# Placing VectorE's small steps by weight in a hand-planned two-layer transformer kernel

## The chip, the cores and the metric

One core of a Trainium2 chip. The metric is the device time in microseconds of one execution; the kernel before took 1615.34 us (median of three runs).

## The reference, cut to what matters

Input x is (4, 1024, 128) float32. There are two layers; each adds an attention branch and a feed-forward branch to x, and both branches read the same layer norm. Layer 0: rotary attention (16 heads of 8), and a mixture of 8 experts with the top 2 per token. Layer 1: causal attention without rotation, and a feed-forward whose inputs and weights are rounded blockwise (blocks of 16) to the FP4 grid.

```python
xn = _layernorm(x, axis=-1)
x = x + _L0_attn_ref(xn, ...) + _L0_ffn_ref(xn, ...)   # softmax(QK^T/sqrt(8))V Wo; top-2 of 8 experts, 128->512->128
xn = _layernorm(x, axis=-1)
x = x + _L1_attn_ref(xn, ...) + _L1_ffn_ref(xn, ...)   # causal; fp4(silu(fp4(xn) Wg) * (fp4(xn) Wu)) Wd
```

## The kernel before, in words

The work is cut into eight **phases** (layer, batch): (0,0) (0,1) (1,0) (0,2) (1,1) (0,3) (1,2) (1,3), numbered 0 to 7. A phase's attention is a row of **steps** (head group g of four heads, half qh of the queries, key tile kt of 128): 64 in a layer-0 phase, 48 in a causal one. Beside the steps run **quads**, 12 slots ahead of them and so often already of the next phase: they compute the same scores the other way round, only to find each query's maximum.

A class `Plan` (lines 42 to 325) writes the whole program out by hand before anything is emitted, as a list of **slots**. One slot holds at most one step, one quad, the product with V of the step before ("pv"), and lists of extra pieces. Every engine walks through the same slots in order:

- TensorE: two heads of the step's scores and of the quad's, the eight matmuls of pv into the bank pO, the other two heads, then the extra pieces ("xs"). All results but pO's go into a ring of seven PSUM banks; TensorE waits until the bank it wants has been emptied. All matmuls are emitted by the helpers on lines 521 (matmul) and 524 (transpose).
- ScalarE: exp of the four score tiles (L833), and its share of the xs copies.
- VectorE: two maxima (L1180 in full, L1184 with the causal mask), the small steps of positions 0 and 1, two maxima, at the end of a head group the combination of the maxima (L1416 to L1419), the small steps of position 2, its share of the xs evictions, the small steps of position 3.
- GpSimd: in order, rstd (L731), sum, rem and lo of the split of Q and K into three bf16 parts (L738, L742, L746), eight rounding operations of the FP4 step at two a slot (L790 to L810), scatter and gather of the expert rows (L763, L779).
- SyncE: all other DMAs, in slot order, each with its waits.

**Extra pieces (xs)**, by who evicts them. ScalarE: xT (transposed norm), v, unit and y (the two matmul layers of one expert tile of 128 tokens), xqT and turn (transposes of the FP4 input), of, cT, wT. VectorE: pj (Q, K projections; a and b with rotation, L1436, L1438), lg and rt (gates and routing), mtr (transposed maxima), fin (division by the softmax sum, L1456 to L1463), gu (gate and up, L1468, L1472), down and fp (added to x, L1480). mtr and fin have fixed slots (`force`); most others go through `put`, which takes the first of three slots that has no xs, else the first with fewer than two.

**Small steps** of VectorE are placed by `chain`, one position of four per slot after another, so that four usually fall in one slot: stats (two bn_stats, L1230), means (four bn_aggr, L1234) and var; norm (two tiles, L1247, after rstd from GpSimd); the routing steps; comb (the experts' rows times their weight added to x, L1360); xq and hq, the four VectorE steps of an FP4 chain (L1393 to L1405).

`prepare(p, at)` places the layer norm, transposes, projections, stores and loads of phase p, and the routing (layer 0) or the feed-forward (layer 1: xq, gu, hq, turn, down). After an hq chain comes |y| on ScalarE (L943), then four slots with two GpSimd rounding operations each, then turn and down; the next hq starts after that, so one chain takes six slots. `tiles(p)` places scatter, the 23 expert tiles, gather and comb. `finish(p)` places cT, of and fp. The order of the calls matters, since each one sees what was put before it: for p = 0 to 7 finish, tiles (layer 0), then prepare(p + 1). Phase 3 is prepared from slot 168, phase 5 from slot 280 (two slots after the start of the phase before them), phases 2, 4, 6 and 7 one slot after the comb of the expert phase that they build on (slots 135, 223, 334, 397). The last step is in slot 485; the last slot is 490.

Of the kernel before, what the change touches and what calls it, by code (L numbers as in the profile page):

```python
# [9 lines left out]
TH = HALF // P  # L10
# [3 lines left out]
T = 8  # L14
NH = 2
# [15 lines left out]
W_STEPS, W_FIRST, X_STEPS = 12, 7, 4  # L31
POOL_STEPS = 8


class Plan:
# [8 lines left out]
    def __init__(self):  # L44
# [31 lines left out]
        for p, (layer, b) in enumerate(PHASES):  # L76
            if layer == 0:
                self.finish(p)
                if p:
                    self.tiles(p)  # L80
            else:
                self.finish(p)
            if p + 1 < len(PHASES):
                if PHASES[p + 1][0] == 0:
                    self.prepare(p + 1, self.start[p] + 2 if p else self.gated[p] + 2 * T + 2)
                    if p == 0:
                        self.tiles(p)
                else:
                    lead = max(self.start[p], self.done[PHASE_OF[0, PHASES[p + 1][1]]]) + 1
                    self.prepare(p + 1, lead)  # L90
# [5 lines left out]
    def slot(self, i):  # L96
# [3 lines left out]
        return self.slots[i]  # L100

    def force(self, i, event):
        self.slot(i)["xs"].append(event)
        return i

    def put(self, i, event, most=0):

        if not most:
            for k in range(3):
                if not self.slot(i + k)["xs"]:  # L110
                    return self.force(i + k, event)
            most = 2
        while len(self.slot(i)["xs"]) >= most:
            i += 1
        return self.force(i, event)

    def chain(self, key, i, steps, every=1):
        place = max(self.place.get(key, 0), 4 * i)
        at = []
        for e in steps:  # L120
            self.slot(place // 4)["small"][place % 4].append(e)
            at.append(place // 4)
            place += every
# [23 lines left out]
    def tiles(self, p):  # L147
# [24 lines left out]
        for k in range(2):  # L172
            for t in range(T):
                i = max(i, j + 2)
                self.slot(i + t // 2)["pool"].append(("gather", p, k, t))
            i = self.chain("comb", i + T // 2 + 1, [("comb", p, k, h) for h in range(NH)], 2)[-1] + 1
        self.done[p] = max(self.done.get(p, 0), i + 1)
# [12 lines left out]
    def prepare(self, p, at):  # L190
        layer, b = PHASES[p]
        if layer == 0 and b:
            self.slot(max(0, at - 3))["sp"].append(("x", b))
        i = self.chain("ln", at, [("stats", p, t) for t in range(0, T, 2)]
                       + [("means", p, t) for t in range(0, T, TH)] + [("var", p)])[-1]
        self.slot(i)["pool"].append(("rstd", p))
        i = self.chain("ln", i + 1, [("norm", p, t) for t in range(0, T, 2)])[-1]
        for h in range(NH):
# [39 lines left out]
        else:  # L238
            for h in range(NH):
                j = self.chain("fp4", first + 1, [("xq", p, h, k) for k in range(X_STEPS)])[-1]  # L240
                i = max(i, self.rounding(j + 1, ("xq", p, h)))
                i = self.put(i + 1, ("xqT", p, h))
            for t in range(T):
                i = self.put(i + 1, ("gu", p, t, 0))
                i = self.put(i, ("gu", p, t, 1))
                j = self.chain("fp4", i + 1, [("hq", p, t, k) for k in range(X_STEPS)])[-1]
                k = self.rounding(j + 1, ("hq", p, t))
# [16 lines left out]
    def number(self):  # L264
# [6 lines left out]
        for s in self.slots:  # L271
# [17 lines left out]
            for e in s["xs"]:  # L289
                who = "D" if e[0] in ("pj", "lg", "rt", "mtr", "fin", "gu", "down", "fp") else "A"  # L290
                k = len(self.xs)
# [25 lines left out]
def two_layer_block(nc, x, wqa0, wqb0, wka0, wkb0, wv0, wo0, gate_w, gate_b, w1, b1, w2, b2wo,  # L317
# [26 lines left out]
    with ctx:  # L344
# [221 lines left out]
        with nc.Block() as block:  # L566
# [580 lines left out]
            def _(dve):  # L1147
# [71 lines left out]
                def small_step(e):  # L1219
# [132 lines left out]
                    if kind == "comb":  # L1352
# [5 lines left out]
                        own()  # L1358
                        for t in range(TH * h, TH * h + TH):
                            ins = v.scalar_tensor_tensor(xr[b % NX][:, t, :], yg[:, D * t:D * t + D], pr[b % 2][:, i, t:t + 1],  # L1360
# [177 lines left out]
```

## Time and profile before

| | us |
|---|---|
| median of three runs | 1615.34 |
| the runs | 1614.98, 1615.34, 1619.94 |
| the profiled execution | 1609.59 |
| its span, first to last instruction | 1607.9 |
| busy in the span: TensorE, VectorE | 1459.2, 1338.0 |
| busy in the span: ScalarE, GpSimd | 1129.9, 576.2 |

The span is what the trace covers; the execution's own time is 1.7 us longer. In the rows below PE is TensorE, DVE VectorE, ACT ScalarE, POOL GpSimd, SP SyncE, and PEclk or "granted clock" the share of full speed at which TensorE was clocked (0.5 is 1.2 GHz, 1.0 is 2.4 GHz). In a row of windows the busy times stand in the order PE, PEld (weight loads), DVE, ACT, POOL. "Idle before" is the engine's idle time ahead of an instruction, and the name after the arrow is what ended it.

### The profile page before, as it was taken

To read this page: it belongs to the slowest core of one execution; us is meant where nothing else is said; L and a number is where in the kernel's file an instruction comes from. 1 tells how busy PE (TensorE), PEld (TensorE's weight loads), DVE (VectorE), ACT (ScalarE), POOL (GpSimd) and SP (SyncE) were. 2 spreads that over 40 slices of the span, in tenths; PEclk is the share of its full clock that TensorE was granted. 3 is DMA by queue.
4 is the path that set the end of the run, shared out by engine and by line. 5 is a ranking of instruction groups with operands and counts; after the bars stand their busy time and mean duration, and the time that the engine had idled before them with its cause. 6 is when DMAs were issued, how large, how long until landed. Compare 5 with 4: busy or idle time off the path is not lost.

```text
span 1607.9 us, 34216 instructions
## 1 busy us (share of the span) xinstructions
PE 1459.2 (91%) x10557; PEld 582.2 (36%) x10557; DVE 1338.0 (83%) x3450; ACT 1129.9 (70%) x2580; POOL 576.2 (36%) x531
## 2 busy tenths in 40 slices
PE   3978999999999999989999999999999988899986
PEld 1112344443334453433333444333444323323322
DVE  6999877789887888898998778889888878888880
ACT  2167678788788577778878557777878845765675
POOL 3002302103244646424444451230623564543520
PEclk8599999999999999999999889999999988999999
DMA  6303273333362253323511135142742101500000
GB/s 173 100 8 99 65 185 116 105 87 92 95 162 65 76 145 88 89 78 100 125 35 51 48 93 141 52 113 78 185 104 79 34 19 46 114 2 15 2 2 14
DMA packets 169833, 131.84 MB, mean 82 GB/s; under 512 B 31597, under 2 KB 143158, under 8 KB 169654
## 3 DMA queue, kind: packets, MB, share of 16 engines
q1 hardware_dynamic: 165562, 121.26, 28.6%
q0 software_dynamic: 4096, 8.40, 1.8%
q8 instruction: 91, 1.49, 0.4%
q14 instruction: 84, 0.69, 0.1%
HBM read 88.50 MB, written 40.50 MB: 80 GB/s over the span
## 4 chain that ended last, share of the span: by engine, by line
PE 60%; DVE 23%; issue 7%; ACT 5%; POOL 2%; DMA 2%; SPq 1%; DVEq 0%; ACTq 0%; POOLq 0%
PE ring L521 38%; PE pO L521 18%; DVE mparts L1180 13%; PE ring L524 4%; ACT PR L833 3%; DVE junk L1184 2%; DVE xr L1360 1%; DVE stats L1230 1%; DVE xn L1247 1%; ACT hid L904 1%; DVE hs L1468 1%; POOL rstd L731 1%; DVE msplit L1418 1%; DVE hs L1472 0%; ACT parts L527 0%
## 5 line engine op out<-in xcount | busy, mean ns | idle before, releaser
L833 ACT ACTIVATE PR<-ring 128x512 f32<-128x512 f32 (+3 forms) x1792 | 881.9, 557 | 331.4 <-PE ring L521 327.4
L1180 DVE TENSOR_REDUCE mparts<-ring 128x1 f32<-128x512 f32 x1280 | 807.4, 682 | 87.1 <-PE ring L521 78.5
L521 PE MATMUL ring<-QX,KX 50*128 50x512 bf16 (+3 forms) x1792 | 541.6, 367 | 75.6 <-DVE mparts L1180 34.2
L521 PE MATMUL ring<-KX,QX 48*128 48x512 bf16 (+3 forms) x1792 | 555.8, 374 | 14.2 <-DMA QX<-scratch 14.1
L521 PE MATMUL pO<-PR,VX 128*18 128x512 f32 (+3 forms) x3584 | 446.9, 572 | 9.4 <-ACT PR L833 8.2
L521 PEld LDWEIGHTS ring<-QX,KX 50*128 50x128 bf16 x1792 | 126.0, 94 | 606.4 <-ACT PR L833 208.3
L1184 DVE CUSTOM_DVE_ANT_0 junk<-ring,diag 128x384 bf16<-128x384 f32 (+3 forms) x512 | 228.3, 486 | 48.6 <-PE ring L521 45.6
L790 POOL TENSOR_SCALAR bq<-bq 128x352 f32<-128x352 f32 (+1 forms) x40 | 47.1, 1177 | 324.7 <-ACT bq L943 324.5
L763 POOL DMA_INDIRECT rows_in<-xn,at x64 | 62.6, 978 | 257.3 <-PE pO L521 172.1
L521 PEld LDWEIGHTS ring<-KX,QX 48*128 48x128 bf16 x1792 | 125.8, 94 | 33.6 <-DVE mparts L1180 17.9
L904 ACT ACTIVATE hid<-ring,b1r 128x128 f32<-128x128 f32 x368 | 105.1, 370 | 25.0 <-PE ring L521 23.9
L779 POOL DMA_INDIRECT ra<-rows_out,at x64 | 61.5, 961 | 149.7 <-PE pO L521 102.5
L521 PE MATMUL ring<-yx,w1r 128*128 128x128 f32 x736 | 107.5, 290 | 6.6 <-DMA b1r<-in_b 3.4
L521 PEld LDWEIGHTS pO<-PR,VX 128*18 128x18 f32 x3584 | 60.7, 97 | 135.9 <-issue 87.1
L521 PEld LDWEIGHTS ring<-yx,w1r 128*128 128x128 f32 x736 | 91.4, 195 | 33.2 <-DVE mparts L1180 23.6
L521 PE MATMUL ring<-w2r,hid 128*128 128x128 f32 x736 | 98.6, 277 | 0.0
L521 PEld LDWEIGHTS ring<-w2r,hid 128*128 128x128 f32 x736 | 94.4, 199 | 0.9 <-DVE mparts L1184 0.5
L521 PE MATMUL ring<-identb,laterb 128*128 128x128 bf16 x512 | 75.8, 232 | 0.0
L746 POOL TENSOR_TENSOR parts<-rb,parts 128x512 bf16<-128x512 f32 x30 | 34.6, 1155 | 76.6 <-ACT parts L527 76.6
L804 POOL TENSOR_SCALAR yq<-yq 128x352 f32<-128x352 f32 (+1 forms) x40 | 60.4, 1510 | 3.3
L799 POOL TENSOR_TENSOR bq<-hq,bq 128x352 f32<-128x352 f32 x64 | 59.7, 933 | 4.7
L527 ACT ACTIVATE yx<-ring 128x256 f32<-128x256 f32 (+1 forms) x96 | 36.2, 377 | 35.5 <-PE ring L521 33.2
(165 smaller groups left out, 1345.8 us busy)
## 6 DMA issues: line engine op xcount, KB each, us to landing
w1r<-in_w SPq DMA_DIRECT2D x92, 256.0 KB
w2r<-in_w SPq DMA_DIRECT2D x92, 256.0 KB
scratch<-parts SPq DMA_DIRECT2D x48, 256.0 KB, 3.3
scratch<-parts SPq DMA_DIRECT2D x96, 128.0 KB, 2.4
KX<-scratch SPq DMA_DIRECT2D x64, 192.0 KB, 4.4
QX<-scratch SPq DMA_DIRECT2D x128, 96.0 KB, 4.5
xg<-rows_in SPq DMA_DIRECT2D x92, 64.0 KB
rows_out<-yx SPq DMA_DIRECT2D x92, 64.0 KB
```

The source lines that it names most:

```text
L521: return nc.tensor.matmul(dst, lhsT, rhs, start=start, stop=stop, **kw)
L524: return nc.tensor.transpose(dst, src, ident[0:src.shape[0], 0:src.shape[0]])
L527: return nc.scalar.activation(dst, src, ACT.Copy)
L763: nc.gpsimd.indirect_dma_start(xs[b % 2], bass.IndirectOffsetOnAxis(at[b % 2][:, c:c + 1], 0), xn[0][:, c % T, :], None).then_inc(s_sc[b], 16)
L779: nc.gpsimd.indirect_dma_start(yg[:, D * t:D * t + D], None, ys[b % 2], bass.IndirectOffsetOnAxis(at[b % 2][:, c:c + 1], 0)).then_inc(s_yg ...
L790: ins = nc.gpsimd.tensor_scalar(b_, b_, 1.0, None, ALU.max)
L799: ins = nc.gpsimd.tensor_tensor(b_, dst, b_, ALU.subtract)
L804: ins = nc.gpsimd.tensor_scalar(y, y, SHIFT, SHIFT, ALU.add, ALU.subtract)
L833: nc.scalar.activation(PR[:, n % 2, HALF * j + off:HALF * j + HALF], ring[plan.bank("E", k)][:, off:HALF], ACT.Exp, scale=SCALE).then_inc( ...
L904: ins = nc.scalar.activation(hid[N % 2][:, P * fc:P * fc + P], src[:, P * fc:P * fc + P], ACT.Relu, bias=b1r[N % 2][:, fc:fc + 1])
L1180: v.tensor_reduce(dst, src[:, 0:w], axis=X, op=ALU.max).then_inc(s_mr, 1)
L1184: v.tensor_tensor_reduce(out=junk[k % 2][:, 0:w], in0=src[:, 0:w], in1=diag[:, HALF - w:HALF], scale=1.0, scalar=NEG, op0=ALU.add, op1=ALU ...
```

## The change

Only the planner changes, and the grain of the combine step. No arithmetic is added or removed.

- Each kind of xs and of small step gets a weight (`HEAVY`, `SMALL`). `busy(i, who)` adds up what slot i already holds for VectorE ("D") or ScalarE ("A").
- `put`: of the same three slots it now takes the first without xs in which weight and piece come to at most 14 (a heavier piece counts as 14), then the first without xs up to 99 (a heavier piece by its own weight), and only then the old rule.
- `chain` gets a `room`: a step that would bring a slot that isn't empty over it goes to the next slot. Statistics and norms of phases 3 to 6 have room 18, xq likewise, hq has 16 in phases 2 and 4; all others have none.
- Phases 3 and 5 are prepared from 20 slots before the start of the phase ahead of them instead of two after it.
- comb is cut into four pieces of two tiles instead of two of four: in phases 1 and 3 at every second position (two slots), in 0 and 5 at every position (one slot).

```diff
+ON_VECTOR = ("pj", "lg", "rt", "mtr", "fin", "gu", "down", "fp")
+HEAVY = {"unit": 24, "y": 6, "turn": 11, "xT": 10, "v": 11, "cT": 10, "xqT": 10, "of": 10, "wT": 10,
+         "pj": 11, "mtr": 8, "fin": 15, "gu": 8, "down": 5, "fp": 11, "lg": 5, "rt": 5}
+SMALL = {"stats": 9, "means": 10, "norm": 12, "best": 5, "which": 8, "hits": 7, "comb": 12, "rem": 11, "wq": 15,
+         "xq": 9, "hq": 6}
...
-                    self.prepare(p + 1, self.start[p] + 2 if p else self.gated[p] + 2 * T + 2)
+                    self.prepare(p + 1, self.start[p] - 20 if p else self.gated[p] + 2 * T + 2)
...
+    def busy(self, i, who):
+        s = self.slot(i)
+        xs = sum(HEAVY[e[0]] for e in s["xs"] if (e[0] in ON_VECTOR) == (who == "D"))
+        return xs + (sum(SMALL.get(e[0], 3) for q in s["small"] for e in q) if who == "D" else
+                     6 * (len(s["act"]) + len(s["late"])) + (10 if s["out"] else 0))
...
         if not most:
-            for k in range(3):
-                if not self.slot(i + k)["xs"]:
-                    return self.force(i + k, event)
+            who = "D" if event[0] in ON_VECTOR else "A"
+            for room in (14, 99):
+                for k in range(3):
+                    if not self.slot(i + k)["xs"] and self.busy(i + k, who) + min(HEAVY[event[0]], room) <= room:
+                        return self.force(i + k, event)
...
-    def chain(self, key, i, steps, every=1):
+    def chain(self, key, i, steps, every=1, room=0):
...
+            while room and self.busy(place // 4, "D") and self.busy(place // 4, "D") + SMALL.get(e[0], 3) > room:
+                place = 4 * (place // 4 + 1)
...
-            i = self.chain("comb", i + T // 2 + 1, [("comb", p, k, h) for h in range(NH)], 2)[-1] + 1
+            i = self.chain("comb", i + T // 2 + 1, [("comb", p, k, h) for h in range(T // 2)], 2 if p in (1, 3) else 1)[-1] + 1
...
+        room = 18 if 3 <= p <= 6 else 0
         i = self.chain("ln", at, [("stats", p, t) for t in range(0, T, 2)]
-                       + [("means", p, t) for t in range(0, T, TH)] + [("var", p)])[-1]
+                       + [("means", p, t) for t in range(0, T, TH)] + [("var", p)], 1, room)[-1]
...
-        i = self.chain("ln", i + 1, [("norm", p, t) for t in range(0, T, 2)])[-1]
+        i = self.chain("ln", i + 1, [("norm", p, t) for t in range(0, T, 2)], 1, room)[-1]
...
-                j = self.chain("fp4", first + 1, [("xq", p, h, k) for k in range(X_STEPS)])[-1]
+                j = self.chain("fp4", first + 1, [("xq", p, h, k) for k in range(X_STEPS)], 1, room)[-1]
...
-                j = self.chain("fp4", i + 1, [("hq", p, t, k) for k in range(X_STEPS)])[-1]
+                j = self.chain("fp4", i + 1, [("hq", p, t, k) for k in range(X_STEPS)], 1, 16 if p < 6 else 0)[-1]
...
-                        for t in range(TH * h, TH * h + TH):
+                        for t in (2 * h, 2 * h + 1):
```

## Rows read from the trace of the kernel before

**Rows 1.** The page: busy time, and the chain that ended last, by engine.

```profile
PE 1459.2 (91%) x10557; PEld 582.2 (36%) x10557; DVE 1338.0 (83%) x3450; ACT 1129.9 (70%) x2580; POOL 576.2 (36%) x531
...
PE 60%; DVE 23%; issue 7%; ACT 5%; POOL 2%; DMA 2%; SPq 1%; DVEq 0%; ACTq 0%; POOLq 0%
```

**Rows 2.** Windows by stage: length, busy us (instructions), PEclk, DMA share, GB/s.

```profile
443.50:511.90 68.40, 65.78 (x483) 25.96 (x481) 56.52 (x172) 57.49 (x126) 33.94 (x28) 1.00 0.48 116
511.90:607.20 95.30, 90.88 (x728) 46.07 (x726) 81.75 (x281) 61.15 (x163) 47.90 (x43) 1.00 0.42 111
...
681.50:746.60 65.10, 57.29 (x389) 20.05 (x387) 59.35 (x133) 49.68 (x104) 17.03 (x16) 0.97 0.29 83
...
859.70:897.10 37.40, 36.01 (x272) 14.13 (x270) 28.46 (x121) 31.46 (x71) 17.05 (x16) 1.00 0.25 69
897.10:957.60 60.50, 57.31 (x377) 28.62 (x375) 44.38 (x145) 30.45 (x82) 32.62 (x29) 0.84 0.20 59
957.60:1068.80 111.20, 103.31 (x847) 43.65 (x846) 92.75 (x267) 79.02 (x196) 23.10 (x24) 0.97 0.38 101
1068.80:1140.40 71.60, 66.71 (x487) 29.50 (x486) 62.42 (x138) 58.70 (x133) 25.35 (x21) 1.00 0.38 107
...
1300.10:1351.70 51.60, 44.21 (x303) 16.54 (x302) 43.82 (x146) 23.13 (x60) 25.69 (x24) 0.77 0.04 10
...
1390.60:1569.00 178.40, 160.37 (x1267) 54.96 (x1265) 153.20 (x500) 118.44 (x281) 68.97 (x65) 0.95 0.09 19
1569.00:1597.00 28.00, 20.27 (x181) 5.43 (x181) 1.14 (x6) 19.58 (x48) 0.00 (x0) 1.00 0.00 1
```

**Rows 3.** Timeline of VectorE, 717 to 728 us: start, us, what.

```profile
722.58 1.11 DVE L1247 TENSOR_SCALAR xn<-xr,mv,rstd 128x128 f32<-128x128 f32 x4
723.60 2.47 DVE L1180 TENSOR_REDUCE mparts<-ring 128x1 f32<-128x512 f32 x4
```

**Rows 4.** TensorE, 717 to 730 us; in brackets idle before and releaser.

```profile
724.34 0.23 PE L521 MATMUL ring<-identb,msplit 128*32 128x128 bf16 x1 [1.87 <-DVE mparts L1180]
```

**Rows 5.** VectorE by line and form, whole span: busy, mean ns | idle.

```profile
L1247 DVE TENSOR_SCALAR xn<-xr,mv,rstd 128x128 f32<-128x128 f32 x64 | 22.6, 415 | 5.2 <-POOL rstd L731 5.1
L1360 DVE SCALAR_TENSOR_TENSOR xr<-ra,pr,xr 128x128 f32<-128x128 f32 x64 | 20.2, 376 | 1.5 <-DMA ra<-rows_out,at 1.5
...
L1472 DVE SCALAR_TENSOR_TENSOR hs<-th,ring 128x352 f32<-128x352 f32 x32 | 16.6, 519 | 23.6 <-ACT th L918 22.0 <-DVE xr L1480 0.8 <-issue 0.7
L1405 DVE SCALAR_TENSOR_TENSOR yq<-hs,ri 128x352 f32<-128x352 f32 x32 | 16.6, 519 | 0.8
...
L1393 DVE TENSOR_REDUCE am<-hs 128x22 f32<-128x352 f32 x32 | 16.4, 511 | 0.0
...
L1230 DVE BATCH_NORM_STATS2 stats<-xr 128x6 f32<-128x128 f32 x64 | 15.4, 283 | 4.8 <-DMA xr<-in_x 3.7
...
L1401 DVE RECIPROCAL ri<-sc 128x22 f32<-128x22 f32 x32 | 9.0, 282 | 0.0
...
L1234 DVE BATCH_NORM_AGGREGATE mv<-stats 128x2 f32<-128x6 f32 x64 | 6.0, 156 | 0.3
```

**Rows 6.** Busy time and granted clock in two stretches of slots 281 to 290.

```profile
912.00:925.00 13.00, 13.00 (x63) 5.28 (x64) 8.21 (x24) 4.76 (x11) 6.02 (x5) 0.53 0.00 1
...
952.50:963.00 10.50, 10.50 (x63) 6.84 (x61) 6.26 (x29) 4.38 (x10) 4.07 (x4) 0.56 0.48 138
```

**Rows 7.** Timeline of all engines, 948 to 950 us.

```profile
948.81 0.69 DVE L1436 TENSOR_TENSOR ra<-ring,rc 128x512 f32<-128x512 f32 x1 [3.02 <-POOL parts L746]
...
949.65 0.21 PE L521 MATMUL ring<-QX,KX 50*128 50x128 bf16 x1 [1.01 <-DVE ra L1436]
```

**Rows 8.** Instructions by line and form, GpSimd, 897.1 to 957.6 us.

```profile
L738 POOL TENSOR_TENSOR ra<-ra,rb 128x512 f32<-128x512 f32 x4 | 5.1, 1270 | 15.6 <-DVE rb L1438 15.6
...
L746 POOL TENSOR_TENSOR parts<-rb,parts 128x512 bf16<-128x512 f32 x4 | 4.6, 1155 | 0.7 <-ACT parts L527 0.7
...
L731 POOL TENSOR_TENSOR rstd<-var,minus_half 128x8 f32<-128x8 f32 x1 | 1.7, 1667 | 3.3 <-DVE var L1237 3.3
```

More of the change, by code:

```diff
@@ L289, in number @@
             for e in s["xs"]:
-                who = "D" if e[0] in ("pj", "lg", "rt", "mtr", "fin", "gu", "down", "fp") else "A"
+                who = "D" if e[0] in ON_VECTOR else "A"
                 k = len(self.xs)
```

## The prediction

> **What bounds the kernel now.** Engines first: TensorE 91% busy, VectorE 83%, and the chain of waits runs over TensorE for 60% of the span and VectorE for 23% [rows 1]. So TensorE sets the pace, and VectorE interrupts it. Then the busy time by stage, cut where a slot begins (a slot is found in the trace by counting the eight pO matmuls of each; the slot numbers are 145, 166, 190, 214, 232, 266, 278, 290, 326, 345, 390, 402, 414 and 474 for the 14 cuts in order of time) [rows 2]. There one sees three things. VectorE's load is uneven: 5.8 us idle in 681.5 to 746.6, 16.1 in 897.1 to 957.6. TensorE is less busy just where a layer norm is prepared (57.3 of 65.1, 66.7 of 71.6). And the granted clock falls there too: 0.84 in 897.1 to 957.6.
>
> The cause of the second is in the timeline of 717 to 728: in slot 226 four maxima stand in a row behind four norms [rows 3], and TensorE, whose score matmuls need the ring banks that these maxima empty, sits 1.87 us with "DVE mparts" as releaser [rows 4]. A burst of small steps therefore costs TensorE time although VectorE has room a few slots further on.
>
> **What each part costs.** The sum is made against the profiled execution, 1609.6 us (span 1607.9 and 1.7 around it). The median of the runs, 1615.34, is 5.7 us more; I add that at the end. All placements below are worked out from the planner's rules, so they may be off by a slot or two.
>
> One preparation has 8 bn_stats of 283 ns, 8 bn_aggr of 156 and 8 norms of 415 [rows 5]: 2.3 + 1.2 + 3.3 = 6.8 us. Before they fill three slots; afterwards, for phases 3 to 6, two stats, one means or one norm stand in a slot, and slots with a gu, mtr or fin are skipped, so they take eight to sixteen slots. For phases 3 and 5 they also start 22 slots sooner (146 and 258 instead of 168 and 280). For phases 4 and 6 the start moves back by two slots and the end by eight to ten: "sooner" holds for two preparations of seven.
>
> *Phase 5.* 6.8 us of VectorE work leave 897.1 to 957.6 for slots 258 to 276, where VectorE is idle 8.9 us in slots 266 to 277 alone [rows 2]. Cost there: 0 to 2 us, I take 1. Gain at the old place: between 0 (TensorE is 95% busy) and 6.8; I take 5, as the stage lasts 5.0 us a slot against 3.1 in the one before it. The clock: 13 us at 0.53 and 10.5 us at 0.56 [rows 6] are 12.2 and 9.2 us at the low level (1.2 instead of 2.4 GHz), worth half, 6.1 and 4.6. The first stretch begins in slot 281, where the last layer-0 output projection (fp), four bn_aggr, a gu and the norms' wait meet. Bounds 0 and 10.7; I take the first alone, 6. Together **-10**.
>
> *Phase 3.* The same 6.8 us, and the eight projection evictions of 0.69 [rows 7] (5.5 us) with their transposes and matmuls, move from slots 168 to 178 to about 147 to 169. The old stage has 13.6 us of idle VectorE, the new one 11.9 [rows 2], and TensorE's part is a transfer between two stages that are 95% and 96% busy. Bounds: +3 (both stages on TensorE, some crowding) and -12.3. Nearest is the lower end, since TensorE is so busy in both: **-4**. The x load goes 22 slots sooner on SP's queue; for batch 3 it waits for the output of batch 0, stored at slot 218, long before 255: nothing. V's copy waits for the last product of phase p-2, in slots 166 and 278; by my placement it stands at about 172 and 283, so no wait.
>
> *Phases 4 and 6.* TensorE is idle 7.8 us in 681.5 to 746.6 and 4.9 in 1068.8 to 1140.4 [rows 2]; waits like [rows 4] are part of it. These stages also hold the combine steps of phases 1 and 3: 16 of 376 ns each [rows 5], four in a row before, two afterwards, over twice as many slots. Bounds 0 and the whole idle time; I take somewhat under half: **-3** and **-2**. Their feed-forward quantization starts some 18 and 14 slots later, since it follows the norms; for phase 4 that is into 957.6 to 1068.8, which has 18.4 us of idle VectorE, so I cost it at nothing. That cover is gone if this stage comes up against VectorE.
>
> *The quantization steps (hq).* One chain is mainly 511 + 282 + 519 ns = 1.3 us [rows 5]. In phases 2 and 4 it stands in one slot before, in two or three afterwards. It is shorter than a norm burst, but each of the 16 chains gets one or two slots longer, and turn and down fall more often beside an mtr. Bounds 0 and +6 (16 chains, each later by a fraction of a slot); **+2**.
>
> *The end.* Phase 6's and 7's quantization is pushed back by about 14 slots, phase 7's last down from slot 468 to about 482. Two chains (hq 1.3 and two gu evictions of 0.52: 2.3 us of VectorE each [rows 5]) leave 1390.6 to 1569, where VectorE is 86% busy, for 1569 to 1597, where it does 1.1 us and TensorE 20.3 of 28 [rows 2]. Bounds 0 and -4.7; **-3**.
>
> *Weights of other pieces* (v, wT in the prologue a slot later, some unit and y away from slots with an output copy), the combine of phases 0 and 5 (same slot, smaller pieces): one slot of shift each, nothing.
>
> Sum: -10 -4 -3 -2 +2 -3 = -20. 1609.6 - 20 = 1589.6; with the 5.7 that lie between this execution and the median, **1595**.
>
> **Rivals.**
> *TensorE decides everything.* No instruction is added or removed but for order; if the 91% is real work, moving VectorE's steps is hidden: about 1615. For it: 0.96 busy in 443.5 to 511.9. Against: the 1.87 us of [rows 4] and the low clock. Chance 0.14. The Trainium skill, Perfetto Trace Analysis, Identifying the Most-Contended Engine, says to work on the engine with the highest occupancy, which speaks against this change, but also that matmul busy time is no measure of TensorE's headroom; by its first half the time would be 1615, by its second the question is open.
>
> *GpSimd's queue becomes late: slower.* Each layer-0 preparation gives GpSimd four triples sum, rem, lo of 1.27 + 1.16 + 1.16 us (rem is an operation like lo) = 14.3 us; in 897.1 to 957.6 two roundings share its queue, (32.6 - 14.3 - 1.7) / 2 = 8.3 us each [rows 2, 8]. VectorE already waited 3.02 us for "POOL parts" there, and TensorE 1.01 us for VectorE [rows 7]. By my placement the four triples of phase 3 fall in slots 164 to 170 and a rounding in 166 to 169. In four slots of 3.3 us there are 13.2 us, for 22.6 of work: 9.4 us late, and a low clock behind it as at 952.5 (4.6). Then phase 3 costs +14 instead of -4, and with phase 5's gain (-10) lost the same way the sum is +8: 1623. It decides where a rounding and three or more triples meet inside four slots. Against it: before, the triples at 173 to 180 also met a rounding. Chance 0.14.
>
> *The clock gains more.* 51.6 us from 1300.1 have a clock of 0.77 [rows 2]: 23.7 us low, worth up to 11.9. Phase 6's quantization leaves part of these slots to others, and if this stretch and both of phase 5's stay high, the sum is -20 -11.9 -4.6 = -36: 1579. Chance 0.12.
>
> **How the numbers follow.** The forecast has 0.60, the rivals 0.14, 0.14 and 0.12. A measurement of this kernel can tell about 0.3% (4.8 us) from no change. All best bounds together make -47, all worst ones +11; as the terms will not all err one way, the forecast's own range goes half way to each: -34 to -4, which is 1582 to 1611; to hold 8 in 10 I reach to 1572 and 1620. Faster: nearly all of the forecast's 0.60 and the 0.12, 0.70. Same: most of the first rival and a little of the forecast's edge, 0.15. Slower 0.15.
>
> **What would show it.** In the changed profile: around the start of slots 226 to 240 no run of four norms, and no TensorE wait above 1 us for "DVE mparts"; a granted clock above 0.9 in slots 278 to 289 and fewer than 4.5 us a slot there; VectorE idle below 6 us in slots 266 to 277; VectorE busy by more than 5 us after the last maximum. The forecast is wrong if the number of low-clock stretches stays the same, or if "DVE ra <- POOL parts" waits grow past 3 us in slots 164 to 170; if slots 278 to 289 stay near 60 us, term one has failed.

## The result: 11 us faster, half of the forecast

The changed kernel took 1605.65 us (median of six runs, 1599.19 to 1608.81) against 1616.87 for the kernel before on the same chip (six runs): a ratio of 0.9922, 95% interval 0.9895 to 0.9949. The forecast was 1595 (from 1615.34, a ratio of 0.987), its range 1572 to 1620. So sign and range held; the size was 0.8% where 1.25% was forecast. The profiled execution took 1606.22 us, with a span of 1604.5; before they were 1609.6 and 1607.9. It is only 3.4 us faster than its counterpart, while the medians differ by 11.2: the two profiles lie at the slow and at the fast side of their kernels, so a difference of 4 us in them proves nothing. (Five kernels that run the same program up to slot 145 reach it after 443.0 to 447.5 us.) One run of 1755.01 us of the kernel with free pieces by count, one of 6766.15 us of the kernel with phases 4 and 6 alone, and one of 1964.78 us of the kernel before stand far from all others and are left out of every median, ratio and interval below.

The page of the kernel after: busy time, TensorE's clock in 40 slices, and the chain that ended last.

```profile
PE 1459.2 (91%) x10557; PEld 583.9 (36%) x10557; DVE 1338.2 (83%) x3450; ACT 1129.7 (70%) x2580; POOL 578.4 (36%) x531
...
PEclk8599999999999899999999999999999977989998
...
PE 58%; DVE 26%; issue 6%; ACT 5%; POOL 3%; DMA 1%; SPq 0%; another core or an unknown queue 0%; DVEq 0%; ACTq 0%; POOLq 0%
```

Busy times are those of [rows 1] to 2.2 us: nothing was added or removed. The chain leans a little more on VectorE (26% for 23%) and less on TensorE.

Windows of the kernel after, cut at the slots of [rows 2] (145, 166, 190; 214, 232; 266, 278, 290, 326, 345; 390, 402, 414, 474, and from there a stretch of 28 us, as long as the last row of [rows 2]); columns as in [rows 2].

```profile
443.60:516.20 72.60, 68.69 (x499) 27.71 (x499) 62.93 (x200) 59.40 (x129) 29.47 (x23) 1.00 0.48 117
516.20:612.50 96.30, 89.97 (x699) 45.59 (x698) 72.20 (x250) 57.77 (x155) 46.89 (x44) 0.95 0.42 107
687.40:747.50 60.10, 53.80 (x389) 20.01 (x387) 56.09 (x121) 45.80 (x99) 18.00 (x17) 0.97 0.26 74
860.40:897.60 37.20, 35.70 (x262) 12.92 (x260) 29.11 (x125) 31.62 (x70) 16.68 (x16) 1.00 0.20 55
897.60:941.40 43.80, 43.25 (x349) 20.95 (x348) 35.20 (x114) 27.41 (x74) 14.77 (x14) 1.00 0.12 34
941.40:1063.10 121.70, 113.73 (x906) 50.26 (x905) 106.48 (x302) 85.08 (x212) 68.85 (x65) 0.99 0.39 104
1063.10:1127.10 64.00, 60.27 (x456) 26.09 (x454) 59.03 (x130) 52.22 (x117) 15.84 (x16) 1.00 0.32 90
1288.40:1339.30 50.90, 44.38 (x293) 17.09 (x292) 39.89 (x128) 21.86 (x58) 27.94 (x28) 0.77 0.06 17
1339.30:1384.50 45.20, 41.45 (x286) 15.34 (x284) 40.35 (x122) 29.21 (x70) 21.30 (x20) 0.89 0.18 53
1384.50:1564.30 179.80, 162.03 (x1272) 56.54 (x1270) 155.58 (x505) 119.82 (x282) 85.81 (x75) 0.95 0.12 27
...
1564.30:1592.30 28.00, 23.27 (x197) 7.86 (x195) 4.17 (x13) 21.02 (x53) 14.34 (x14) 1.00 0.01 1
```

Line by line against [rows 2] the stages read +4.2, +1.0, -5.0, -0.2, **-16.7**, **+10.5**, -7.6, -0.7, then +1.4; slots 402 to 413, which stood in no row before, took 1390.6 - 1351.7 = 38.9 and now 45.2, +6.3. The last row has the length that it was cut to. The whole end, from slot 474 to the last instruction, took 1607.9 - 1569.0 = 38.9 us and now 1604.5 - 1564.3 = 40.2, +1.3. What the reader is to see: the large gain of slots 278 to 289 is real there (the clock goes from 0.84 to 1.00) but two thirds of it are lost again right behind, in slots 290 to 325, where VectorE has 13.7 us more to do. The other stages that took in moved work are longer too: 402 to 413 with quantization steps, 145 to 189 with phase 3's preparation.

VectorE and TensorE around slot 226, as in [rows 3] and [rows 4]: first VectorE, then the waits of TensorE in slots 223 to 231.

```profile
719.67 5.11 DVE L1201 TENSOR_REDUCE mparts<-ring 128x1 f32<-128x512 f32 x8
725.32 1.29 DVE L1201 TENSOR_REDUCE mparts<-ring 128x1 f32<-128x512 f32 x2 [0.54 <-PE ring L542]
726.52 1.00 DVE L1251 BATCH_NORM_STATS2 stats<-xr 128x6 f32<-128x128 f32 x4
727.44 1.27 DVE L1201 TENSOR_REDUCE mparts<-ring 128x1 f32<-128x512 f32 x2
```

```profile
PE ring L542 <- DVE mparts L1201: 1.9, 4, 0.6
PE ring L542 <- ACT PR L854: 1.3, 3, 0.5
```

The burst of norms is gone, and the longest wait of TensorE for a maximum is 0.6 us where it was 1.87. (Lines of the kernel after are those of before plus 21.)

The prices of the moved steps, as in [rows 5], and the clock in part of slots 282 to 286, as in [rows 6]:

```profile
L1381 DVE SCALAR_TENSOR_TENSOR xr<-ra,pr,xr 128x128 f32<-128x128 f32 x64 | 24.3, 420 | 0.3
L1268 DVE TENSOR_SCALAR xn<-xr,mv,rstd 128x128 f32<-128x128 f32 x64 | 22.2, 401 | 4.3 <-POOL rstd L752 4.2
L1426 DVE SCALAR_TENSOR_TENSOR yq<-hs,ri 128x352 f32<-128x352 f32 x32 | 17.5, 547 | 0.6
```

```profile
912.50:925.00 12.50, 12.08 (x115) 5.76 (x114) 10.26 (x34) 9.45 (x26) 3.05 (x3) 1.00 0.12 36
```

An instruction costs what it cost (401 for 415 ns, 420 for 376, 547 for 519), and the low stretch of 912 to 925 is gone.

### The profile page after: what moved, and what is told of

Same layout as the page of the kernel before. It is cut to its first block, busy times and chain, and to the rows that moved or that the text cites. A ratio compares the mean times of both kernels' runs of the same rounds, so it can differ in the third digit from the quotient of the medians.

```text
span 1604.5 us, 34217 instructions
## 1 busy us (share of the span) xinstructions
PE 1459.2 (91%) x10557; PEld 583.9 (36%) x10557; DVE 1338.2 (83%) x3450; ACT 1129.7 (70%) x2580; POOL 578.4 (36%) x531
## 4 chain that ended last, share of the span: by engine, by line
PE 58%; DVE 26%; issue 6%; ACT 5%; POOL 3%; DMA 1%; SPq 0%; another core or an unknown queue 0%; DVEq 0%; ACTq 0%; POOLq 0%
PE ring L542 38%; PE pO L542 17%; DVE mparts L1201 15%; PE ring L545 3%; ACT PR L854 3%; DVE junk L1205 2%; DVE xr L1381 1%; DVE stats L1251 1%; ACT hid L925 1%; DVE hs L1493 1%; DVE xr L1501 1%; DVE am L1414 1%; DMA b1r<-in_b 1%; ACT parts L548 0%; DVE hs L1489 0%
## 5 line engine op out<-in xcount | busy, mean ns | idle before, releaser
L542 PEld LDWEIGHTS ring<-KX,QX 48*128 48x128 bf16 x1792 | 127.3, 94 | 33.6 <-DVE mparts L1201 17.9
```

The costliest lines, as they stand in the source:

```text
L542: return nc.tensor.matmul(dst, lhsT, rhs, start=start, stop=stop, **kw)
```

## The experiments

All kernels were run in twelve or six runs beside the kernel before on the same chip. A ratio compares a kernel with the runs of before that stood beside it; it lies up to 0.16% below the quotient of the two medians, inside the interval each time. "Undone" kernels are the changed one with one part taken back, "alone" kernels are the one before with one part added. The last columns split the difference of the mean time from before's mean by the clock: within each kernel, from run to run, the time rises by 0.60 us for each us of (1 - mean granted clock) x span (correlation 0.88 over 226 runs of 14 kernels); "clock" is that slope times the difference in (1 - clock) x span, "rest" is what remains. Before's mean is taken over its 96 runs on three chips, which by themselves have means of 1614.9, 1617.7 and 1619.9 us; so up to 3 us in these two columns can be the chip's. The ratios are free of that.

```
kernel                                  median   ratio    95%              clock   rest
changed                                1605.65   0.9922   0.9895-0.9949     -7.9   -4.7
undone: phase 3's sooner start         1622.45   1.0037   1.0011-1.0064     +3.7   +0.2
undone: weights of free pieces         1597.73   0.9887   0.9858-0.9917     -4.1  -15.9
undone: hq's room                      1612.55   0.9977   0.9954-1.0000     -1.1   -4.4
undone: phase 5 (start and spreading)  1602.76   0.9915   0.9887-0.9943     -2.8  -11.2
undone: spreading of phases 4 and 6    1617.40   0.9977   0.9946-1.0007     +2.5   -4.2
undone: weights and phase 5            1616.75   0.9979   0.9957-1.0001     -0.3   -0.9
alone:  phase 5                        1617.02   0.9983   0.9961-1.0004     -1.9   +0.3
alone:  combination in four pieces     1624.96   1.0040   1.0021-1.0058     +2.6   +4.7
alone:  phase 3                        1620.49   1.0016   0.9999-1.0032     +0.3   +2.7
alone:  hq's room                      1625.61   1.0047   1.0031-1.0064     -0.4   +8.3
alone:  spreading of phases 4 and 6    1618.50   0.9989   0.9967-1.0012     -1.3   +1.1
changed, one rounding four slots later 1605.65   0.9908   0.9885-0.9931     -4.5   -8.7
```

### Parts taken back

**Phase 3 late again**, but still spread:

```diff
-                    self.prepare(p + 1, self.start[p] - 20 if p else ...)
+                    self.prepare(p + 1, self.start[p] + (2 if p == 2 else -20) if p else ...)
```

> The changed kernel, but phase 3 is prepared from slot 168 again (statistics and norms still spread). Theory: phase 3's early start cost time, because its four sum, rem, lo triples met a rounding on GpSimd in slots 164 to 170 and the clock fell (slots 166 to 177 grew from 49.8 to 58.2 us). So slots 166 to 177 fall to about 48 and the whole comes to about 1600, ratio near 0.989. Rival (the early start is neutral, the time only sits elsewhere): 1604 to 1607, ratio 0.992 to 0.994, with the same us appearing in slots 178 to 213, where the projections now fall. Second rival (the early start was the gain): 1610 or more.

It undid the gain and more: 1.0037 against 0.9922, 1.15% or 19 us, far outside both intervals. The stages say how. Windows of this kernel, slots 166 to 189 and 190 to 213:

```profile
515.50:598.80 83.30, 81.78 (x657) 39.05 (x655) 67.31 (x226) 53.66 (x143) 27.36 (x25) 0.94 0.20 55
598.80:689.10 90.30, 84.47 (x624) 37.41 (x622) 78.20 (x211) 61.35 (x151) 51.74 (x48) 0.98 0.41 108
```

Slots 166 to 189 gain 13.0 us on the changed kernel, but 190 to 213 lose 15.4 (90.3 for 74.9), since the spread norms end in slot 188 and the projections now fall in slots 191 to 195, on top of phase 2's quantization and the expert tiles. Another 5.2, 4.9 and 6.8 us are lost in 214 to 231, 278 to 289 and 290 to 299. The local part of the theory held (slots 166 to 177 took 44.5 us), its conclusion did not: the second rival was right. So the sooner start is what pays for the spreading: without it the spreading of phase 3 is a delay. Whether the sooner start would do as well with the steps in bursts was not run.

**Free pieces by count again.** The old rule of `put` for pieces without a fixed slot (86 of 551 pieces move):

```diff
-            who = "D" if event[0] in ON_VECTOR else "A"
-            for room in (14, 99):
-                for k in range(3):
-                    if not self.slot(i + k)["xs"] and self.busy(i + k, who) + min(...) <= room:
-                        return self.force(i + k, event)
+            for k in range(3):
+                if not self.slot(i + k)["xs"]:
+                    return self.force(i + k, event)
```

> The changed kernel with the old rule for extra pieces (first of three slots without one, no weights). Theory: the weights of the pieces move few of them and none on the path, so within 3 us of the changed kernel, ratio 0.990 to 0.994. Rival (weights keep ScalarE's and VectorE's heavy pieces off loaded slots and are part of the gain): 1609 or more, ratio 0.995 or above.

0.9887, the fastest kernel of this study: 0.35% less than the changed one, some 6 us. The two intervals overlap, so a gain over the changed kernel is likely and not shown; that the weights bring no gain worth naming here is.

**hq whole again:**

```diff
-    j = self.chain("fp4", i + 1, [("hq", p, t, k) for k in range(X_STEPS)], 1, 16 if p < 6 else 0)[-1]
+    j = self.chain("fp4", i + 1, [("hq", p, t, k) for k in range(X_STEPS)], 1, 0)[-1]
```

> The changed kernel, but the four steps of an hq chain stand in one slot again in phases 2 and 4, so a chain takes 6 slots instead of 8. Theory: spreading hq costs a little, as the later chains crowd the slots of phases 3 and 5's preparation: 1 to 4 us faster than the changed kernel, ratio 0.990. Rival (VectorE's room is the bound and spreading hq is a part of the gain): 3 to 6 us slower than the changed kernel, ratio 0.995 to 0.997.

0.9977: 0.55% or 9 us of the gain gone, against the theory and more than its rival had. The part that I had costed at +2 is worth -9 in company. **Phase 5 as before**, late and in bursts:

```diff
-                    self.prepare(p + 1, self.start[p] - 20 if p else ...)
+                    self.prepare(p + 1, self.start[p] + (2 if p == 4 else -20) if p else ...)
-        i = self.chain("ln", i + 1, [("norm", p, t) for t in range(0, T, 2)], 1, room)[-1]
+        i = self.chain("ln", i + 1, [("norm", p, t) for t in range(0, T, 2)], 1, 0 if p == 5 else room)[-1]
```

(and the same for the statistics)

> The changed kernel, but phase 5's statistics and norms stand in three slots at 280 to 282 as before. Theory: the gain in slots 278 to 289 (60.5 to 43.8 us) came from this one preparation, and with it a stretch at the low clock; it goes: slots 278 to 289 back to 55 to 60 us, the whole about 1615, ratio 0.998 to 1.0. Rival (the stall came from the hq, turn and gu pieces that now stand elsewhere, not from the norms): slots 278 to 289 stay below 50 us and the whole within 4 us of the changed kernel.

0.9915 against 0.9922: no difference, where the two intervals together could hide some 6 us. Yet slots 278 to 289 are back at 56.1 us with a clock of 0.88. Most of the 12.3 us lost there are made up by slot 390, for slots 290 to 389 take 336.3 us instead of 347.0. Slots 278 to 289 and 290 to 389 of this kernel, then 290 to 389 of the changed one:

```profile
895.10:951.20 56.10, 53.32 (x368) 26.20 (x366) 42.19 (x141) 30.01 (x79) 23.83 (x22) 0.88 0.18 54
951.20:1287.50 336.30, 323.38 (x2443) 137.35 (x2441) 294.32 (x732) 266.25 (x616) 139.44 (x127) 0.99 0.37 98
```

```profile
941.40:1288.40 347.00, 328.61 (x2467) 140.43 (x2466) 294.37 (x735) 268.46 (x620) 145.05 (x131) 0.99 0.37 99
```

It is not that VectorE has less left to do there: it is busy 294.3 us in the one and 294.4 in the other, at the same clock. TensorE is busy 5.2 us less and idle 5.5 us less. Why is open. **Phases 4 and 6 in bursts:**

```diff
-        room = 18 if 3 <= p <= 6 else 0
+        room = 18 if p in (3, 5) else 0
```

> The changed kernel, but statistics, norms and xq of phases 4 and 6 stand in bursts again. Theory: the gain goes: 1612 to 1618, ratio 0.998 to 1.002, with slots 326 to 344 back at 70 us or more. Rival (the other parts carry it): 1605 to 1608, ratio 0.993 to 0.995.

0.9977, another 9 us gone, as the theory had it. Slots 214 to 231 take 65.5 us again and 326 to 344 take 69.9: the two local gains belong to this part.

### Parts alone

Five kernels, each the one before with one part. **Phase 5**, sooner and spread; **phase 3**, the same with `p == 2` and `p == 3`:

```diff
-                    self.prepare(p + 1, self.start[p] + 2 if p else ...)
+                    self.prepare(p + 1, self.start[p] + (-20 if p == 4 else 2) if p else ...)
-        i = self.chain("ln", i + 1, [("norm", p, t) for t in range(0, T, 2)])[-1]
+        i = self.chain("ln", i + 1, [("norm", p, t) for t in range(0, T, 2)], 1, 18 if p == 5 else 0)[-1]
```

> The kernel before with one part alone: phase 5 prepared from slot 258, its statistics and norms spread (room 18). Theory A (the norm burst of phase 5 made the 60.5 us of slots 278 to 289): that stage falls by 10 us or more and the whole by 8 to 12, ratio 0.993 to 0.995. Theory B, from the run that put the burst back into the changed kernel and lost nothing: the burst is harmless and the stall comes from the low clock, which this part meets by chance: within 3 us of the kernel before, ratio 0.998 to 1.002.

> The kernel before with one part alone: phase 3 prepared from slot 147, its statistics and norms spread (room 18). Theory, from the run without this part (16 us slower than the changed kernel): the early start is the main gain: 6 to 14 us faster than before, ratio 0.991 to 0.996, with slots 178 to 213 shorter. Rival (it was needed only because hq, spread over more slots, fills slots 168 to 213): within 3 us of before.

**The combination in four pieces:**

```diff
-            i = self.chain("comb", i + T // 2 + 1, [("comb", p, k, h) for h in range(NH)], 2)[-1] + 1
+            i = self.chain("comb", i + T // 2 + 1, [("comb", p, k, h) for h in range(T // 2)], 2 if p in (1, 3) else 1)[-1] + 1
-                        for t in range(TH * h, TH * h + TH):
+                        for t in (2 * h, 2 * h + 1):
```

> The kernel before with one part alone: the combine steps in four pieces of two tiles, over two slots in phases 1 and 3 (all that follows in phases 4 to 7 moves back two slots). Theory: 2 to 4 us faster by shorter bursts in slots 214 to 222 and 325 to 333, ratio 0.998. Rival (only the order of the rest matters, and two slots shift it at random): anything from 6 us slower to 6 us faster, with the difference outside those slots.

**hq's room:**

```diff
-                j = self.chain("fp4", i + 1, [("hq", p, t, k) for k in range(X_STEPS)])[-1]
+                j = self.chain("fp4", i + 1, [("hq", p, t, k) for k in range(X_STEPS)], 1, 16 if p < 6 else 0)[-1]
```

> The kernel before with one part alone: hq spread (room 16) in phases 2 and 4. Theory, from the run that took this part out (7 us slower than the changed kernel): it relieves slots with four small steps: 3 to 7 us faster than before, ratio 0.996 to 0.998. Rival (it helps only where phase 3 is prepared early, and otherwise crowds slots 168 to 213): 2 to 8 us slower, ratio 1.001 to 1.005.

**Spreading of phases 4 and 6** (statistics, norms and, as here, xq):

```diff
-                j = self.chain("fp4", first + 1, [("xq", p, h, k) for k in range(X_STEPS)])[-1]
+                j = self.chain("fp4", first + 1, [("xq", p, h, k) for k in range(X_STEPS)], 1, 18 if p in (4, 6) else 0)[-1]
```

> The kernel before with one part alone: statistics, norms and xq of phases 4 and 6 spread (room 18), which no run so far has undone. Theory: this is where the gain lies, since slots 214 to 231 and 326 to 344 are 5 and 7 us shorter in the changed kernel and stay so in all its variants: 6 to 12 us faster than before, ratio 0.993 to 0.996, with the rest at full clock lower by as much. Rival (no part gains alone; only together do they shift the later phases into a better order): within 3 us of before or slower.

None gains beyond its interval. Three of the rivals named the size: phase 3, hq's room and phases 4 and 6 stayed where their rivals had them; phase 5 stayed where theory B had it. The combination came out slower (0.40%, 6 to 8 us) than both its texts allowed; in its profile slots 232 to 265 and 402 to 413 are 4.8 and 7.8 us longer, 390 to 401 6.7 us shorter. The five deviations from 1 add up to -0.17 + 0.40 + 0.16 + 0.47 - 0.11 = **+0.75%** (root sum of the half widths 0.4), while the five together, which is the kernel with free pieces by count, have **-1.13%** (0.3). The difference, 1.9% or 30 us, belongs to no part.

The trace of phases 4 and 6 alone shows where a part gives its gain back. With phases 4 and 6 alone, slots 214 to 231 fall from 65.1 to 56.0 us and 326 to 344 from 71.6 to 63.9, as in the whole. But the quantization that comes later fills slots 290 to 325 (125.7 us for 111.2), and slots 390 to 413 take 97.7 for 90.5. One of the new waits, in slot 390, where half of phase 5's combination, four hq steps and a turn have come together (columns: engine, line, releaser, us in total, times, longest):

```profile
PE ring L539 <- POOL hq L825: 5.6, 1, 5.6
```

Slots 390 and 391 take 10.0 and 5.5 us. In the whole change the combination stands in slots 392 and 398, apart from hq. With hq's room alone slots 402 to 413 take 48.8 us at a clock of 0.81, where they took 38.9.

### Together again, and GpSimd's queue

**Weights and phase 5 both undone**, the two edits above in one kernel:

> The changed kernel with the two parts undone that cost or gave nothing when each was undone by itself: the free pieces go into slots by count again, without weights (undone alone: ratio 0.9887), and phase 5 is prepared late and in bursts as before (its bursts alone restored: 0.9915, the same as the whole change's 0.9922). What stays are phase 3 begun sooner, the spread statistics and norms of phases 3, 4 and 6, hq's room in phase 4 to 6 and the combination in pieces. Theory 'the gain is that of phases 3, 4 and 6 and of hq, and the rest may go': the parts' effects add, so 0.9887 plus or minus 0.002, about 1598 us, with slots 278 to 289 back at 55 us or more and slots 300 to 325 back near 75. Rival 'the parts only work together': phase 5's early start is what keeps the clock up between slots 278 and 289, and with both undone the time is back within 0.3% of before, 1612 or more, with more than 115 us at the low clock.

The rival's number was right. By addition the ratio would have been 0.9887 + 0.9915 - 0.9922 = 0.9880; it was 0.9979 (0.9957 to 1.0001), 1.0% or 16 us more, outside the joint error of some 0.5%. It has 119.7 us at the low clock, its slots 278 to 289 take 56.5. So phase 5's sooner start is worthless beside the weighted pieces and worth 15 us (0.9887 against 0.9979) beside the counted ones. The reason that the rival gave is not borne out in size: by the table the clock carries about 4 of these 15 us. In the profiles 10.5 of them stand in slots 278 to 289 (56.5 for 46.0) and 9.2 in 345 to 389 (165.4 for 156.2). What has a price here is a whole schedule.

**One rounding behind phase 3's triples.** This is the rival of the forecast, tested in its own place:

```diff
+        if what == ("hq", 2, 1):
+            i = max(i, 169)
```

(at the place where that chain's rounding operations are put; it moves from slots 166 to 169 to slots 170 to 173)

> The changed kernel, with phase 2's second rounding on GpSimd moved from slots 166 to 169 to slots 170 to 173, behind phase 3's four triples of sum, remainder and low part; nothing else is edited, but the later chains of phase 2's quantization shift by some five slots with it. Theory 'GpSimd's queue is what makes the early start of phase 3 dear': the wait of the scalar engine for GpSimd (2.46 us) and TensorE's 2.11 us behind it in slot 167 go, the granted clock stays above 0.9 in slots 167 to 169, slots 166 to 177 take 50 to 53 us and not 58.2, and the whole is 4 to 6 us less than the changed kernel's, a ratio to before near 0.989. Rival 'the low clock there comes from the small matmuls that slot 169 holds': the wait goes, but slot 169 still takes 10 us or more at a clock below 0.8, slots 166 to 177 stay at 56 or more, and the ratio stays at 0.992 or above.

GpSimd in slots 166 and 167 of the changed kernel: a split's sum, two rounding operations, a lo, a rem, two roundings, a lo, without a gap.

```profile
516.88 1.27 POOL L759 TENSOR_TENSOR ra<-ra,rb 128x512 f32<-128x512 f32 x1 [1.84 <-DVE rb L1459]
518.11 1.09 POOL L811 TENSOR_SCALAR bq<-bq 128x352 f32<-128x352 f32 x1
519.29 1.09 POOL L817 TENSOR_SCALAR hq<-bq 128x352 f32<-128x352 f32 x1
520.35 1.16 POOL L767 TENSOR_TENSOR parts<-rb,parts 128x512 bf16<-128x512 f32 x1
521.47 1.15 POOL L763 TENSOR_TENSOR rb<-ra,parts 128x512 f32<-128x512 f32 x1
522.59 1.93 POOL L820 TENSOR_TENSOR bq<-hq,bq 128x352 f32<-128x352 f32 x2
524.48 1.16 POOL L767 TENSOR_TENSOR parts<-rb,parts 128x512 bf16<-128x512 f32 x1
```

And who waited for it, in the same kernel between 516.2 and 544.3 us (engine, what, releaser: us in total, times, longest); then, from the timeline, the matmul that came late:

```profile
ACT parts L548 <- POOL rb L763: 4.4, 2, 2.5
...
PE ring L542 <- ACT PR L854: 3.4, 2, 2.1
```

```profile
523.81 0.32 PE L542 MATMUL ring<-QX,KX 50*128 50x384 bf16 x1 [2.11 <-ACT PR L854]
```

ScalarE stands 2.5 us in front of its copy "parts", the exp behind it in its queue is late, and TensorE finds no empty bank. Windows of slots 166, 167, 168 and 169 of the changed kernel, and then of this one:

```profile
516.20:520.40 4.20, 4.20 (x30) 1.43 (x31) 1.90 (x11) 3.56 (x7) 3.44 (x4) 1.00 0.00 1
520.40:528.70 8.30, 6.19 (x35) 3.65 (x34) 3.83 (x14) 3.40 (x9) 5.16 (x5) 0.79 0.61 192
528.70:533.00 4.30, 4.30 (x41) 2.27 (x41) 2.71 (x10) 2.60 (x7) 3.93 (x3) 1.00 0.00 0
533.00:544.30 11.30, 10.03 (x41) 4.79 (x41) 5.93 (x16) 1.41 (x5) 4.37 (x6) 0.71 0.46 128
```

```profile
518.10:522.30 4.20, 4.20 (x28) 1.43 (x27) 1.90 (x12) 3.57 (x7) 3.50 (x3) 1.00 0.00 1
522.30:526.70 4.40, 4.40 (x36) 2.23 (x34) 3.64 (x14) 3.41 (x9) 1.16 (x1) 1.00 0.54 170
526.70:531.00 4.30, 4.30 (x37) 2.24 (x35) 2.71 (x10) 3.19 (x8) 2.44 (x3) 1.00 0.61 197
531.00:537.80 6.80, 6.80 (x46) 3.64 (x48) 5.04 (x16) 1.28 (x5) 1.15 (x1) 1.00 0.64 183
```

The same slots with the same extra pieces: 28.1 us against 19.7, both long slots gone, the clock at 1.00 all through. Slots 166 to 177 fall from 58.1 to 48.1 (in 170 to 177 some of phase 2's pieces have moved on as well). That the rounding causes the stall of these four slots is shown, and the slot with the small matmuls of fp is not slow by itself. The stall is no accident of one execution: the four other kernels in which the same rounding meets the same triples in these slots have 56.6 to 58.1 us in slots 166 to 177. Yet the whole takes the same 1605.65 us (ratio 0.9908 against 0.9922, a difference of 0.14% that is known to 0.36%). By slot 266 the profiles are level again, 859.5 and 860.4 us: slots 178 to 265 took 293.3 instead of 286.1, with 6.8 us at the low clock around slot 250 that the changed kernel did not have there, and the later chains of phase 2 had moved by some five slots. I expected 4 to 6 us of the 10 to remain; the medians show nothing of it, and the intervals would still allow it.

Similar waits stand in slots 278 to 289, but no run moved a rounding there, so what they cost is only argued. Waits of ScalarE there: in the changed kernel, in the one with hq whole, and in the one before.

```profile
ACT parts L548 <- POOL ra L759: 1.8, 2, 1.0
ACT parts L548 <- POOL rb L763: 1.5, 2, 0.9
```

```profile
ACT parts L548 <- POOL rb L763: 7.2, 3, 3.1
ACT parts L548 <- POOL ra L759: 2.4, 3, 1.1
```

```profile
ACT parts L527 <- POOL rb L742: 9.0, 4, 2.8
...
ACT parts L527 <- POOL ra L738: 1.2, 2, 0.7
```

The stage took 43.8, 59.0 and 60.5 us. In the kernel with hq whole phase 5 is prepared sooner as well, but its triples fall in slots 279 to 286 among roundings of phase 4, and slot 281 takes 10.7 us; with phase 5 alone it is the same (slot 281 10.4 us, the stage 57.9). In the changed kernel the one rounding of the stage stands in 285 to 288 and the triples begin in 287 and end behind 289; GpSimd is busy 14.8 us in the stage, for 31.3 with hq whole and 32.6 before.

All profiles together say that this meeting is not the only cause. The seven kernels that prepare phase 5 from slot 280 have 53.4 to 60.5 us in the stage; with phases 4 and 6 alone it is 53.4 us with 13.7 at the low clock, although ScalarE waits only 2.7 us for GpSimd. Of the seven that begin at 258 or 260, the four whose triples begin in slot 287 have 43.8, 46.0, 43.8 and 48.6 us, and the three whose triples fall in 279 to 286 have 51.3, 57.9 and 59.0. So both the late burst and the meeting go with a long stage. And the 60.5 us of before lie at the upper end of what its late start gives: of the 16.7 us gained, some 10 to 17 go with the moved phase.

## Why the prediction was right, and where its sum failed

The sum was -20; the medians give -11 and the two profiled executions -3.4. The code placed most steps as I had worked out, to a slot or two; one placement and several prices failed. And the sign came out with some luck: the sum adds parts by themselves, and the parts by themselves add up to +0.75%, slower. The gain is there only with the parts in company, which no term of the sum had.

*Phase 5, -10.* The old place was right: VectorE has 9.2 us less in slots 278 to 289, the clock at 1.00, 43.8 us (3.65 a slot). The step that failed is "Cost there: 0 to 2 us, I take 1", and with it the placement "eight to sixteen slots", 258 to 276: the room put the four norm steps into slots 269, 273, 277 and 284, so that the preparation takes 27 slots. The work that left did not go only forwards (+0.6 us of VectorE in 266 to 277, idle 8.1 us there and not below 6): the projections stand in 287 to 290, two slots later than before, because the norms are spread to 284, and the gates, routing and hq behind them went to 290 to 325 (+10.5 us). Over 266 to 325 the net is -6.4 in the profiles, and by experiment the part is worth nothing that can be told (0.07%, known to 0.4%) in the changed kernel.

*Phase 3, -4.* The stages 145 to 189 read +5.2, with some 10 us at the low clock (0.95 of 96.3 us, half the clock missing in it), and alone the part costs 0.16%, which its interval does not tell from nothing. This is the rival "GpSimd's queue becomes late" in its place and slots: the triples and the rounding met in 166 to 169, the wait passed through ScalarE and not, as I had it, through VectorE ("DVE ra <- POOL parts" stayed at 0.89 us). But its price was 8.4 us in these four slots and not 9.4 + 4.6 = 14, and in the kernel as a whole nothing that was measured; and it did not take phase 5's gain, as my price assumed.

*Phases 4 and 6, -3 and -2.* The stages moved by -5.0 and -7.6, of the 7.8 and 4.9 us of idle TensorE that were my bounds (the second goes past its bound, as the number of instructions in it fell too). Undoing them costs 9 us. Alone they bring nothing, because of slots 290 to 325 and 390 to 413. "Their quantization goes into 957.6 to 1068.8, which has 18.4 us of idle VectorE, so I cost it at nothing" was wrong: that stage took 10.5 us more with VectorE busy 106.5 of 121.7. Phase 4's quantization not only began later, it was drawn out: its last hq step stands in slot 323 instead of 284.

*hq, +2.* Alone +0.47%, 8 us, above the bound of +6; beside the rest -9. *The combination*, costed at nothing in phases 0 and 5 and as part of the two terms above in 1 and 3: alone +0.40%, 6 to 8 us; the changed kernel without it was not run. *Weights*, costed at nothing: some +6, with the doubt given above.

*The end, -3.* VectorE did move to the tail (4.2 us in 28 for 1.1; the forecast asked for 5), but nothing was cheaper for it. Slots 414 to 473 took 179.8 for 178.4, 402 to 413 6.3 more, and the end from slot 474 on 40.2 for 38.9. The term failed whole.

*The clock.* 117.1 us at the low level behind slot 39 became 100.3 (2 us of each behind the last instruction), in 16 stretches instead of 17 (by the forecast's own test nearly the sign of a failure), and over the runs the mean clock rose from 0.949 to 0.957; by the split above that is -7.9 of the -12.6 between the means. It was the largest single item and I had -6. In the two profiles, though, 10.8 of the 16.8 us fewer at the low clock stand before slot 145 (28.7 and 17.9 us), in a stretch that took 374.1 and 374.4 us; five executions of one and the same program have 18.0 to 32.1 us there. So the profiles cannot show where the change raised the clock, but for slots 278 to 289. I took a low stretch to cost half its length. The run-to-run slope is 0.60 of that, 0.3 us per us at 1.2 GHz. The Trainium skill, TensorE: Matmul & The Clock Gate, Terms, gives the penalty as about the throttled time times (1 - K/N), which is the half that I took; these runs do not bear it out as a size for this kernel. A likely reason, not shown, is that other engines are waited for in part of the low time. (The slope is a correlation over undesigned differences: late engines may lie behind both low clock and length, and it does not tell which came first.) The stretch of slots 390 to 401 stayed at 0.77 exactly, so the rival "the clock gains more" had no ground.

*TensorE decides everything* fell with the first interval: TensorE's busy time is 1459.2 us in both kernels, and the time went by 0.8%. The Trainium skill, Perfetto Trace Analysis, Identifying the Most-Contended Engine, has the engine of highest occupancy worked on first, but does not take matmul busy time as a measure of TensorE's headroom; these runs agree with the exception.

What stays open: which pairs of parts make the 30 us that belong to no part, beyond the two that were shown (phase 3's start with its own spreading, and weights with phase 5), and by what waits; and whether the kernel with counted pieces and the later rounding would gain by both. It wasn't run. Nor was any other order of the steps, chosen without regard to load: the 13 orders that were run spread from 0.9887 to 1.0047, so a gain of 0.8% might also be met without the reasoning behind this one.

## What to carry to other kernels

In a hand-planned schedule a local gain is not a gain: undoing the part that had shortened a stage lengthened that stage by 12.3 us and left the whole time unchanged (to some 6 us), and a stall of 8.4 us could be removed whole without a gain that six runs would show. Price a reordering by the whole plan, with its parts both alone and taken out; a part that costs 8 us alone (hq's room) can be worth 9 in company. Spreading an engine's small steps delays what hangs on them, so begin it sooner too (for phase 3 that was worth 19 us), and then look at which other queue the moved work meets, here GpSimd, whose lateness reaches TensorE by way of ScalarE's queue.

## What the runs showed of the hardware that I had not expected

The same slot with the same matmuls took 11.3 us at a granted clock of 0.71 or 6.8 us at 1.00, with or without a wait of 2.1 us of TensorE two slots earlier and one of 1.3 inside it: here low clock and waits come together. And most of the spread between runs of one and the same kernel (standard deviation 4.4 us over 96 runs of the kernel before) goes with the granted clock: with (1 - clock) x span taken out at 0.60, it falls to 2.3 us.
